# Splitting the weights of a graph network's first layers on GpSimd, ahead of its other work, and a longer VectorE loop in the edge stage

## The reference

```python
# first network: three layers
for l in range(3):
    neigh = segment_sum(h[src], dst, n) * inv_deg
    h = h @ Ws_self[l] + neigh @ Ws_neigh[l] + bs[l]
    if l != 2: h = relu(h)
x = layernorm(x + h)
# second network
e = mlp(edge_attr_4, emb_*)                       # silu, two matrices, layer norm
e_in = concat([e, mesh_nfeat[src], x[dst]])
e_new = mlp(e_in, edge_*) + e
agg = segment_sum(e_new, dst, n)
x2 = mlp(concat([x, agg]), node_*) + x
out = layernorm(x + x2)
```

## Time and profile before

| | |
|---|---|
| median of 3 runs | 2459.51 us (2458.76 to 2459.82) |
| the profiled execution | 2459.82 us |
| its span, first to last instruction | 2458.1 us |
| TensorE busy (matmuls) | 2267.3 us, 92% |
| VectorE busy | 1410.5 us, 57% |
| ScalarE busy | 1180.5 us, 48% |
| GpSimd busy | 1100.8 us, 45% |
| mean granted clock of TensorE | 0.972 |
| start of phase_b's work | 428.4 us |
| end of its last product | 770 us |

### The profile page before, as it was taken

How to read it: one execution, slowest core, us unless ns; L and a number is a source line. 1 busy time by engine, 2 the same in 40 slices (tenths; PEclk the granted TensorE clock), 3 DMA queues, 4 the chain that set the end, 5 groups by cost and what they waited for, 6 DMA issues and landing times. The chain is left out here.

```text
span 2458.1 us, 44265 instructions
## 1 busy us (share of the span) xinstructions
PE 2267.3 (92%) x13412; PEld 1922.2 (78%) x13413; DVE 1410.5 (57%) x3090; ACT 1180.5 (48%) x2123; POOL 1100.8 (45%) x1665
## 2 busy tenths in 40 slices
PE   2988488999986899999999999999999999999897
PEld 1436388777764788888888888888888888888776
DVE  7012288534462566666666666666666666666566
ACT  0121111324311666666666666666666666666421
POOL 4777600000001455555555555555555555555323
PEclk9999799999998899999999999999999999999899
DMA  6223100001123433333233333233333333323121
GB/s 191 78 54 79 19 0 1 34 5 35 35 89 115 133 61 60 63 64 60 60 60 60 64 61 63 60 60 60 63 60 61 62 60 61 63 60 65 24 91 43
DMA packets 76277, 149.67 MB, mean 61 GB/s; under 512 B 14689, under 2 KB 15789, under 8 KB 76219
## 3 DMA queue, kind: packets, MB, share of 16 engines
q0 software_dynamic: 44864, 93.18, 19.8%
q1 hardware_dynamic: 31243, 55.63, 6.8%
q10 hardware_dynamic: 112, 0.11, 0.0%
HBM read 129.12 MB, written 19.46 MB: 60 GB/s over the span
## 5 line engine op out<-in xcount | busy, mean ns | idle before, releaser
L1277 DVE CUSTOM_DVE_ANT_0 c_var_bank<-c_var_bank,c_p,k_floor 128x512 f32<-128x512 f32 x176 | 133.5, 758 | 369.4 <-PE c_var_bank L1434 369.4
L1168 POOL DMA_INDIRECT c_from_src<-s_dst_table,c_at_nodes x176 | 283.8, 1613 | 31.9 <-issue 31.9
L1488 PE MATMUL c_edge_bank<-c_m_hi,c_pt_hi 128*128 128x512 f32 x704 | 291.7, 414 | 0.0
L1489 PE MATMUL c_edge_bank<-c_m_lo,c_pt_hi 128*128 128x512 f32 x704 | 276.8, 393 | 0.0
L1490 PE MATMUL c_edge_bank<-c_m_hi,c_pt_lo 128*128 128x512 f32 x704 | 275.2, 391 | 0.0
L1162 POOL DMA_INDIRECT c_from_src<-s_mesh_table,c_at_nodes x176 | 206.3, 1172 | 152.1 <-POOL c_at_nodes L1158 142.8
L1174 POOL TENSOR_TENSOR c_dev<-c_var,k_half 128x1 f32<-128x1 f32 x176 | 97.8, 556 | 383.9 <-DVE c_var L1264 383.9
L318 POOL DMA_INDIRECT s_records<-a_stage_rec,a_stage_row x170 | 207.3, 1219 | 56.8 <-issue 48.8
L1383 ACT ACTIVATE c_h<-c_from_src 128x512 f32<-128x512 f32 x176 | 111.2, 632 | 249.0 <-DVE c_from_src L1296 249.0
L1432 PE MATMUL c_var_bank<-c_m_hi,c_pt_hi 128*128 128x384 f32 x704 | 226.6, 322 | 4.5 <-ACT c_var_bank L1357 4.5
L1432 PE MATMUL c_var_bank<-c_m_hi,c_ht_hi 128*128 128x384 f32 x704 | 226.8, 322 | 0.0
(11 more groups left out here) (313 smaller groups left out, 6023.0 us busy)
## 6 DMA issues: line engine op xcount, KB each, us to landing
k_w<-in_L_gnn_Ws_self_dram SPq DMA_DIRECT2D x3, 1024.0 KB, 10.1
k_w<-in_L_gnn_Ws_neigh_dram SPq DMA_DIRECT2D x3, 1024.0 KB, 12.8
c_from_src<-s_mesh_table,c_at_nodes POOLq DMA_INDIRECT x176, 3.5
c_from_src<-s_dst_table,c_at_nodes POOLq DMA_INDIRECT x176, 4.7
s_records<-a_stage_rec,a_stage_row POOLq DMA_INDIRECT x170, 2.6
a_mesh<-in_L_gnn_mesh_nfeat_dram SPq DMA_DIRECT2D x10, 250.0 KB
k_h<-in_x_dram SPq DMA_DIRECT2D x1, 2500.0 KB
s_mesh_table<-a_mesh_out SPq DMA_DIRECT2D x10, 250.0 KB
```

The lines of the kernel that those rows point to most:

```text
L1168: pool.indirect_dma_start(from_src[u][:], None, scratch["dst_table"], bass.IndirectOffsetOnAxis(ap=at_nodes[u][:, 1:2], axis=0), compute_o ...
L1277: dve.tensor_tensor_reduce(var1_bank[:], var1_bank[:], p[u % 2][:], 1.0 / D, k["floor"][:, 0:1], ALU.mult, ALU.add, var[u][:, 0:1]).then_i ...
L1488: pe.matmul(edge_bank[:], left[0], m_hi[1][:, c, :], start=False, stop=False, skip_group_check=True)
L1489: pe.matmul(edge_bank[:], left[0], m_lo[1][:, c, :], start=False, stop=False, skip_group_check=True)
```

## The change

The split of the weights for all three rounds of phase_b is made by GpSimd. At the start of round r's part of its stream it waits (r > 0) for the weights and for the end of the products of the round before, copies both high parts, waits for them, and subtracts both low parts. Only when all three rounds' parts are through does it come to the `pow`s. The split of the second layer's weights leaves phase_a and is GpSimd's r = 0; TensorE waits for it ahead of round 0's products. ScalarE and VectorE lose their split operations in both phases. SP loads the next weights into `w` only after `w_split` r, for round 1 too, and waits in phase_a for the second layer's weights itself. Apart from this, VectorE takes `steps` in phase_c.

```diff
@@ phase_a, SP
             sp.wait_ge(mesh_stored[u], 16 * NB // 2)
+        sp.wait_ge(w_next, 32)
         sp.wait_ge(bias_next, 16)
@@ phase_a, VectorE, after the last u_lo
-        for i in range(2):
-            dve.wait_ge(w_next_hi, i + 1)
-            dve.tensor_tensor(w_lo[i][:], w[i][:], w_hi[i][:].bitcast(F32), ALU.subtract).then_inc(w_next_lo, 1)
         dve.wait_ge(recs_in, 16)
@@ phase_a, ScalarE, after the last u_hi
-        act.wait_ge(w_next, 32)
-        for i in range(2):
-            act.activation(w_hi[i][:], w[i][:], ACT.Copy).then_inc(w_next_hi, 1)
@@ phase_b, SP
         for r in range(1, LAYERS):
-            if r > 1:
-                sp.wait_ge(w_split, 2 * r - 2)
+            sp.wait_ge(w_split, r)
@@ phase_b, GpSimd
+        for r in range(LAYERS):
+            if r:
+                pool.wait_ge(w_in, 32 * r)
+                pool.wait_ge(prod_mm, NB * r)
+            for i in range(2):
+                pool.tensor_copy(w_hi[i][:], w[i][:]).then_inc(split_step, 1)
+            pool.wait_ge(split_step, 2 * r + 2)
+            pool.tensor_tensor(w_lo[0][:], w[0][:], w_hi[0][:].bitcast(F32), ALU.subtract)
+            pool.tensor_tensor(w_lo[1][:], w[1][:], w_hi[1][:].bitcast(F32), ALU.subtract).then_inc(w_split, 1)
+
         for i in range(NB):
             pool.wait_ge(var_ok, i + 1)
@@ phase_b, VectorE, in the sums
                 mix(q, i)
-                if q and i in (2, 4):
-                    split(q, i // 2 - 1)
@@ phase_b, ScalarE, in the sums
-                if q and i in (1, 3):
-                    act.wait_ge(w_in, 32 * q)
-                    act.wait_ge(prod_mm, NB * q)
-                    j = i // 2
-                    act.activation(w_hi[j][:], w[j][:], ACT.Copy).then_inc(w_hi_ok, 1)
@@ phase_b, TensorE, multiply
             if i == 0:
-                need(pe, w_split, 2 * r)
+                pe.wait_ge(w_split, r + 1)
@@ phase_c, VectorE
-        short_steps(dve, step)
+        steps(dve, step)
```

More of the change, by code:

```diff
@@ L206, in phase_a @@
     prod_mm, self_ok, u_hi_ok, u_lo_ok = (sem(n) for n in ("prod_mm", "self_ok", "u_hi_ok", "u_lo_ok"))
-    w_next, bias_next, w_next_hi, w_next_lo = (sem(n) for n in ("w_next", "bias_next", "w_next_hi", "w_next_lo"))
+    w_next, bias_next = sem("w_next"), sem("bias_next")
     def spread(b):
@@ L735, in phase_b @@
     many_ok, many_mm, many_read = sem("many_ok"), sem("many_mm"), sem("many_read")
-    w_hi_ok, w_split = sem("w_hi_ok"), sem("w_split")
+    w_split, split_step = sem("w_split"), sem("split_step")
     hc_ok, turned, ht_hi_ok, ht_lo_ok, prod_mm = (
@@ L849, in normalise @@
                                   ALU.subtract, ALU.mult).then_inc(h_ok, 1)
-        def split(r, j):
-            dve.wait_ge(w_hi_ok, 2 * r - 1 + j)
-            dve.tensor_tensor(w_lo[j][:], w[j][:], w_hi[j][:].bitcast(F32), ALU.subtract).then_inc(w_split, 1)
         def multiply(r):
@@ L1100, in steps @@
                 step(GROUPS - 2 + v, v, u)
[L1102 to L1110, removed]
     def at(tensor, n, width=1):
```

## The result

The changed kernel takes 2477.38 us (median of 4, 2475.86 to 2478.02) beside 2459.14 for the kernel before on the same chip: ratio 1.0073, interval 1.0060 to 1.0085. It is slower by 18.2 us, where +8.9 was forecast, and 0.9 us above the range. All sixteen executions of the changed kernel together have a median of 2476.5. The profiled execution took 2471.52 us (span 2469.8), so its trace shows 11.7 of the 18.2; it was the fastest of the sixteen, at a mean granted clock of 0.972 where the others had 0.969 to 0.971.

The account below looks back on a forecast made before the run. TensorE's matmuls bound over half the program; before that, chains of GpSimd, TensorE and VectorE in turn. Terms -2.0 + 7.0 + 0 + 3.9 + 0 = +8.9 gave 2468.4 us, range 2456.5 to 2476.5.

Parts of the forecast that it names:

- the scatter's 2.0: End of phase_a: without VectorE's subtractions beside the scatter, the records land 2.0 us earlier, -2.0.
- GpSimd holds VectorE: phase_b: each two-input VectorE operation stands until the GpSimd operation ahead of it is done; sum +8.9 by this rule.
- The subtraction's 4.6 us: phase_b's moved split: a GpSimd subtraction of 2048 elements a row takes 4.6 us.
- Round 2's +3.9 with nothing won back: phase_b, round 2: first pair normalised at 672.2 instead of 668.30, +3.9, and later pairs no closer together.
- the chain in phase_a and phase_b decides, and the sign: What the change can be worth lies in the first 780 us; the kernel gets slower, sum +8.9.
- The copy: phase_b's moved split: a GpSimd copy of 2048 elements a row takes 1.8 us.
- round 0's term: phase_b's start: the split now made there by GpSimd costs +7.0, bounds 0 and 7.9.
- VectorE first: Round 0 order with VectorE first at the door: TensorE starts 3.3 late, then another 2.9; together 6.2.
- GpSimd first: Round 0 order: the second L807 stands behind both copies and a subtraction; 7.9 at the start, nothing later.
- phase_c's term: phase_c: VectorE's loop of eight tiles a turn for four costs 0, bounds -1.5 and +2.
- More than that: Rival: low clock after each new stall, GpSimd ahead every time, code fetches at the longer loop; +17, 2476.5, chance 0.04.
- second stall or low clock in round 0: Round 0: TensorE out of work again for 2.9; a second low-clock spell after it would add 2.0.

Follow-up runs that it names:

- The run with the late split: The changed kernel with VectorE's four-tile loop back and GpSimd's round 0 held until VectorE's first mix, against the kernel before: 2463.85 us, ratio 1.0025.

## Why the prediction was wrong

*Right:* the scatter's 2.0 (2.1). That GpSimd holds VectorE, which no row of before had shown: 0.83 became 2.55 and 5.07. The subtraction's 4.6 us: 4.49. Round 2's +3.9 with nothing won back (3.2). That the chain in phase_a and phase_b decides, and the sign.

*The copy* was priced 1.8 us; the rows it came from give 1.9 (195 ns for 16 elements and 0.84 ns for each further one), and 1.89 is what a copy takes with nothing ahead of it. That made little.

*The step that failed is round 0's term*, +7.0 with 7.9 as its upper bound, where +11.9 was measured. Both of its orders, VectorE first and GpSimd first, pass over L882, which stands between L878 and the second L807. The prediction counted as held only operations with two SBUF inputs; L882 is a TENSOR_SCALAR with one, and it stood 4.47 us beside the first subtraction. In the trace GpSimd was first at the door, by 0.01 us. By that order the second L807 should have waited at the door during the first subtraction and run in front of the second. But VectorE's queue is in order, L882 was in front of it, and so it came 0.11 us after the second subtraction had begun and was caught by that too: 4.4 us more. The opening ended behind all four GpSimd pieces: four VectorE instructions are longer by 1.7 + 1.6 + 4.3 + 4.3 = 11.9 us (from 0.83, 0.16, 0.16 and 0.81), which is the whole +11.9. The run with the late split shows it from the other side: without GpSimd beside them the four are short again. The Trainium skill's page SBUF — State Buffer, in the section Who interferes with whom, does name this: tensor_scalar, copy and cast can run in modes that take the port pair shared with GpSimd, even with one SBUF input. The trace agrees, 4.47 us for 0.16; the prediction used only the page's sentence on two inputs.

*The second failure is phase_c's term*, 0 with +2 as its bound "for code that has to come in". The loop costs by where it begins: about 3 us in the changed kernel, nothing 88 instructions further on, 60 us 6 further on. The +2 had no row behind it that could bound it. The rival "More than that" came nearest in size (+17), by the low clock, GpSimd ahead in every round and code together; the runs gave the size by the opening and the code, and no second stall or low clock in round 0.

*What is left.* Opening (+4.9) and tiles (+2.9) bring the forecast's sum to +16.7, beside 18.2 measured. That it comes so near is partly luck: in the trace the scatter, the counting and rounds 1 and 2 were 2.75 us below the forecast and the entry of phase_c 1.4 above it. These make the +15.4 that the trace shows without its short end; the last 3 us up to the median lie in executions that left no trace. Which instruction of the loop pays the 0.12 us stays open too.

## What to carry to other kernels

Before work goes to GpSimd, list every VectorE instruction that will run beside it, those of ten elements and those with one input too, and ask what is queued behind each: the same 13 us of GpSimd work cost 11.9 at the opening of a stage and 4.1 one block later. When a loop body has hundreds of instructions, or when phases that an edit doesn't touch move by a few tenths of a per cent, shift the code by a few harmless instructions before judging the edit: here two memsets were worth 5 us in the tiles and six cost 60. Read the queue of instruction packets; it tells a loop that is fetched anew in each turn from one that stays.

## What the runs showed of the hardware

- A loop of 302 VectorE instructions stayed in instruction memory when it began at instruction 801 or 889 (2 to 3 packets in 1350 us) and was fetched again each turn at 807 (92 and 96 packets of 8 KB, about 5 a turn, 3.2 us of program time each turn: 8.986 for 8.581 us a tile). The Trainium skill's page Runtime: NRT & Kernel Launch, in the section Instruction fetch mechanics, says that an engine holds two blocks of 256 instructions and that a taken branch to a target outside them stops it for a fetch. The runs agree in kind: 302 instructions touch two such blocks or three, by where they begin. But counted from the program's first instruction 801, 807 and 889 lie in one block of 256 and their loops all end in the next, and the packets are 8 KB; where the blocks begin no run shows.
- The small effect, 0.14 us in one tile of four, came at 669 and at 797 (and in one tile of eight at 801), and not at 671, 672, 665 or 799: 128 instructions apart it was the same, 2 apart it was gone. In the compiled programs an instruction has 64 bytes, so that 128 are 8 KB, the size of the packets. One pair of places speaks for such steps and doesn't prove them: shorter ones that divide 128, or chance, aren't excluded.
- The hold goes both ways, and in the pairs read here it was whole: in round 1 GpSimd's first subtraction took 5.74 us for 4.49, with VectorE's L824 running ahead of it, and the next L824 stood behind it in turn (2.94 for 1.49). Not every TENSOR_SCALAR is held: L882 with ten elements a partition was (4.47 us), L885 with one, which also began 0.05 us into a subtraction, kept its 0.14. An operation of VectorE that reads PSUM beside SBUF (the mix, 0.75 us) kept its length beside them.
